# Placing the two kinds of attention score units in pairs instead of one by one, on one core

## The reference

```
xn = layernorm(x)
x1 = x + gqa(xn) + block(xn)         # gqa: 16 query heads, 4 key heads, softmax over 512 keys
   block(xn): r = xn + causal latent attention(rmsnorm(xn))     # 16 heads, causal
              r + moe(rmsnorm(r))                                 # 4 experts, 128 -> 512 -> 128, argmax gate
xn1 = layernorm(x1)
out = x1 + mqa(xn1) + gated_ffn(xn1) # mqa: 16 query heads, one key head; silu(gate) * up, 384 wide
```

## Time and profile before

| | |
|---|---|
| median of three runs | 3557.39 us (3550.87 to 3562.95) |
| profiled execution | 3572.11 us, span 3570.4 us |
| TensorE busy | 3302.7 us, 93% |
| VectorE busy | 2421.1 us, 68% |
| ScalarE busy | 1788.8 us, 50% |
| GpSimd busy | 886.0 us, 25% |
| mean granted TensorE clock | 0.914 |

### The profile page before, as it was taken

The page is one execution under the profiler, slowest core; times in us unless marked ns, Lnnn a source line. Parts: engine busy times, 40 slices in busy tenths (PEclk is TensorE's granted clock), DMA queues, the critical chain, the costliest instruction groups (busy, mean ns, idle before and its releaser), DMA issues.

```text
span 3570.4 us, 72884 instructions
## 1 busy us (share of the span) xinstructions
PE 3302.7 (93%) x18176; PEld 1601.2 (45%) x18176; DVE 2421.1 (68%) x5975; ACT 1788.8 (50%) x3505; POOL 886.0 (25%) x1795
## 2 busy tenths in 40 slices
PE   5899999989999899999999999899998989989987
PEld 2354444535445354453544445354453534535443
DVE  5667676676767767676676766767667676766734
ACT  1625545455454545545455454554545545454544
POOL 3232223212222231222222232122321222222110
PEclk8988999989899898998989899898998989989997
DMA  3010101001010100101001010010101001010000
GB/s 95 14 34 18 44 20 43 15 22 35 19 43 18 30 23 19 44 19 41 11 19 46 19 43 14 22 35 19 43 18 30 23 19 43 18 38 14 16 17 4
DMA packets 69679, 99.17 MB, mean 28 GB/s; under 512 B 7708, under 2 KB 30492, under 8 KB 68944
## 3 DMA queue, kind: packets, MB, share of 16 engines
q1 hardware_dynamic: 69200, 93.66, 10.9%
HBM read 8.59 MB, written 4.19 MB: 4 GB/s over the span
## 4 chain that ended last, share of the span: by engine, by line
PE 84%; DVE 5%; issue 4%; ACT 3%; POOL 2%; POOLq 0%; ACTq 0%; DVEq 0%; DMA 0%; SPq 0%
PE pv L701 19%; PE bank L664 16%; PE bank L683 16%; PE bank L739 7%; PE bank L594 7%; PE bank L747 7%; PE bank L710 3%; ACT probs L1101 2%; PE bank L583 2%; DVE mx L902 2%; PE bank L722 1%; PE bank L626 1%; PE bank L764 1%; POOL sq L1179 1%; PE bank L671 1%
## 5 line engine op out<-in xcount | busy, mean ns | idle before, releaser
L1101 ACT ACTIVATE probs<-bank 128x512 f32<-128x512 f32 x2688 | 1474.5, 598 | 1418.4 <-PE bank L683 1412.1
L902 DVE TENSOR_REDUCE mx<-bank 128x1 f32<-128x512 f32 x2048 | 1300.0, 682 | 304.4 <-PE bank L664 296.5
L909 DVE CUSTOM_DVE_ANT_0 bank<-bank,mask 128x128 f32<-128x128 f32 (+3 forms) x1024 | 486.6, 510 | 208.1 <-PE bank L664 199.2
L1265 POOL TENSOR_SCALAR_AFFINE_SELECT probs<-probs 128x256 f32<-128x256 f32 (+1 forms) x640 | 230.2, 361 | 1050.7 <-ACT probs L1101 1044.9
L664 PE MATMUL bank<-kp_B,qp_B 60*128 60x512 f32 x1024 | 360.1, 471 | 47.8 <-issue 38.9
L664 PE MATMUL bank<-kp_A,qp_A 60*128 60x512 f32 x1024 | 367.4, 484 | 11.3 <-DVE mx L902 8.9
L683 PE MATMUL bank<-qp_B,kp_B 62*128 62x512 f32 x1024 | 355.1, 496 | 2.1 <-ACT probs L1101 2.1
L683 PE MATMUL bank<-qp_A,kp_A 62*128 62x512 f32 x1024 | 322.2, 501 | 7.6 <-DVE mx L902 7.2
L701 PE MATMUL pv<-probs,vv_A 128*32 128x512 f32 x2048 | 307.3, 675 | 23.1 <-ACT probs L1101 23.1
L683 PE MATMUL bank<-qp_M,kp_M 62*128 62x512 f32 (+3 forms) x1024 | 293.4, 373 | 36.1 <-DVE mx L902 34.7
L664 PE MATMUL bank<-kp_M,qp_M 60*128 60x128 f32 (+3 forms) x1024 | 299.5, 374 | 12.6 <-DMA kp_M<-parts_k 6.0
(11 more groups left out here) (144 smaller groups left out, 3298.5 us busy)
## 6 DMA issues: line engine op xcount, KB each, us to landing
qp_M<-parts_q SPq DMA_DIRECT2D x64, 256.0 KB, 4.3
kp_M<-parts_k SPq DMA_DIRECT2D x64, 256.0 KB, 4.3
qp_A<-parts_q SPq DMA_DIRECT2D x64, 256.0 KB, 4.6
qp_B<-parts_q SPq DMA_DIRECT2D x64, 256.0 KB, 3.9
kp_A<-parts_k SPq DMA_DIRECT2D x64, 128.0 KB, 2.6
xs<-x SPq DMA_DIRECT2D x16, 256.0 KB, 2.8
out<-res SPq DMA_DIRECT2D x16, 256.0 KB, 2.3
qp_M<-nmT SPq DMA_DIRECT2D x128, 8.0 KB
```

The costliest lines, as they stand in the source:

```text
L902: v.tensor_reduce(mx[:, g % 2, at:at + 1], s1[BANK[a, g, u]][:], AX.X, ALU.max) \
L909: v.tensor_tensor_reduce(bank[:, 0:keys], bank[:, 0:keys], mask[:, SEQ - keys:SEQ], 1.0, LOWEST, ALU.add, ALU.max, mx[:, g % 2, at:at + 1] ...
L1101: act.activation(probs[:, slot, :], s2[BANK2[a, g, u]][:], ACT.Exp).then_inc(sig[f"{a}_exp"], 1)
L1265: pool.affine_select(out=v, in_=v, compare_op=ALU.is_ge, fill=0.0, base=0, pattern=pattern, channel_multiplier=-1).then_inc(sig["M_masked" ...
```

## The change

Two lines of `stages()` give other times to the score units. Units 2k and 2k + 1 now have one time, for the maxima and for the exponentials; nothing else changes in the text of the kernel.

```
-                put(s + g + u / 16, "score_max", a, g, u)
+                put(s + g + u // 2 / 8 + 0.0313, "score_max", a, g, u)
...
-                put(s + LAG + g + (u + 0.5) / n, "score_exp", a, g, u)
+                put(s + LAG + g + (u // 2 * 2 + 0.5) / n, "score_exp", a, g, u)
```

## The result

The changed kernel took 3360.10 us (median of four runs, 3344.44 to 3369.04); the kernel before, now with a fourth run, 3560.17 us (3550.87 to 3580.83). The ratio is 0.943, with a 95% interval from 0.937 to 0.948: 5.7% faster, 200 us. The forecast had 3430 us and a range down to 3365. The sign was right, the size was not: 130 us were expected.

A forecast was written before the change was run, and what follows sets the result against it. TensorE was taken as the bound, fully so in B's group 3 and M's groups. Savings of 6.1 + 2.1 + 0.4 = 8.6 us a period, by 15, made 129 us: 3430 us, range 3365 to 3530.

The forecast's parts named there:

- 0.23 us for a unit on the fuller half: TensorE: each score unit on a run's fuller array half costs 0.23 us; 501 fewer, 115 us at the full clock.
- The price of a run (0.21): TensorE: having a run of score units at all costs 0.21 us; 379 fewer runs, 80 us.
- B's group 3 and M's groups, 6.1 us a period: Five TensorE-bound stretches at full clock: 14 runs and 20.25 units fewer, 7.6 us, taken at 80%.
- The copy of `pv`, taken as 0: ScalarE, A's and B's 8 groups: copy up to 0.5 us later, offset by a removed unit; bounds 0 to 4.0 us.
- The banks: Ring of 7 banks: pairs leave a bank with its reader 0.50 to 0.61 us longer; room enough, covered by the 20% discount.
- The slower rival: Pairs beside `up`, `down` and projections wait 0.5 us each for unread banks, costing more than saved; 3575 to 3626 us, chance 0.09.
- its smaller brother: Readers eat most: 40 maxima pairs in B's group 3 and M's groups cost 4.9 us a period; 3501 us, chance 0.16.
- A's group 1 and B's group 2, 2.1 us: Stretches mostly at low clock or behind latent-norm work: 2.7 us a period saved, taken at 80%.
- the stretches around the seam and the norm, 0: A's groups 2 and 3, B's groups 0 and 1: set by VectorE, seam and norm chain; upper end 1.8 us.
- the clock a risk upwards alone: TensorE idling longer in A's group 0 could prolong the low clock: 1.5 us a period, 22 in all.
- Rival "more than the rows promise", 3345 to 3370, 0.11: Waits at run starts shrink too, since a pair's second unit stands earlier: whole 12.9 us a period or more; chance 0.11.
- Strict order of the matmuls: Rival: matmuls start in program order, so old runs of 4 and 8 lose a step besides; 3326 us, chance 0.02.

The follow-up runs named there:

- same-half variant: Changed kernel with heads taken 0, 2, 1, 3, so both units of a pair are on the same array half: 3621.67 us, 1.016 of the kernel before.
- the two single changes: Kernel before with only the exponentials in pairs: 3509.35 us, 0.984; with only the maxima in pairs: 3502.17 us, 0.983.
- the variants with fewer runs still: Changed kernel with bursts of four: 3585.27 us, 1.004; with exponential pairs moved next to the maxima pairs: 3377.13 us, 0.946.
- the variant with added matmuls: Kernel before with four more matmuls a period ahead of the transposes of x1, where A's group 1 begins: 3549.82 us, 0.995.
- the control: Kernel before with four extra matmuls a period ahead of the transposes of r2, in B's group 3: 3619.06 us, 1.011.
- the woven variant with the late scaling step: Changed kernel with neighbouring exponential and maxima pairs alternating again, and ScalarE's scaling of the normed input 0.05 later: 3429.41 us, 0.962.
- the woven variant: Changed kernel with neighbouring exponential and maxima pairs alternating again on TensorE, halves 0, 0, 1, 1: 3481.53 us, 0.976.

## Why the prediction was wrong

- **TensorE sets the pace, and only its own work counts**: right. TensorE's busy time fell by 257 us, no other engine's work moved much.
- **0.23 us for a unit on the fuller half**: right, 0.22 in the same-half variant. **A pair costs what one unit cost**: right, 1.43 us. The price of a run (0.21) was not isolated, and may be too high: of the two single changes the maxima, with most of their paper saving in runs (53 of 92 us), fell short (67 us), and the variants with fewer runs still were not faster than the changed kernel.
- **B's group 3 and M's groups, 6.1 us a period**: 5.2 measured. M's four groups gave 5.0, B's group 3 only 0.2, with the new wait of 0.56 us ahead of L710. On their own the pairs in these stretches, with A's groups 2 and 3 and B's group 2, gave 94 us.
- **The copy of `pv`, taken as 0**: nearly. TensorE's wait for it rose from 13.9 us (23 times) to 24.1 us (54 times) over the whole, 10 us. This is one of the signs that I had named for being wrong, too small to matter.
- **The banks**: held. The slower rival and its smaller brother did not happen with pairs.
- **A's group 1 and B's group 2, 2.1 us; the stretches around the seam and the norm, 0; the clock a risk upwards alone**: this is the step that failed. A's group 1, and B's groups 0 and 1, gained 9.9 us together; B's group 2 lost 0.7. I priced their saved work at the full clock and took the clock itself as given, or as something that an earlier idle TensorE could only lose. It is an outcome of the order. In the variant with added matmuls the low stretch around A's group 1 ended sooner with more work in it (a mean of 6.3 us for 14.6); in the changed kernel it is 5.9 us, and pairs in the low stretches alone bring it to 6.8. My reading, not tested by itself, is that the same matmuls stand closer together there.
- **What the clock was worth** is an estimate. In A's group 1, the kernel before had 2 x 0.27 x 25.2 = 13.6 us at 1.2 GHz, the variant with added work 2 x 0.10 x 24.5 = 4.9. It did 3.6 us more work in 0.7 us less, 4.3 us for 8.7 us of low clock, or 0.49 each. The changed kernel has 2 x 0.11 x 19.5 = 4.3 us there: 9.3 x 0.49 = 4.6 of its 5.7 us are the clock's, and the other 1.1 are near the 1.3 to 1.6 that its 3 runs and 3 or 4 units are worth on paper. Over the whole, the variant's rate is (41 + 47) / 240 = 0.37 by its profiled span (3529.2 us at 0.947) with the control's 47 us for the work, and 0.40 with 54. With 0.37 to 0.49, the changed kernel's 230 us less at the low clock are worth 84 to 113 us, and 90 to 119 of the 203 us of its profiled span are left for work and waits, where I had 129. So by this estimate the work was sized a little high, and the clock, put at nothing, was about half of the gain.
- **The parts do not add up exactly.** Paper prices for the work (195 us), 0.40 for each us less at the low clock (92) and TensorE's added idle time (54) make 195 + 92 - 54 = 233 us for the changed kernel, where the spans differ by 203. For the pairs of exponentials alone they make 46 + 44 - 42 = 48 for 61, and for the pairs of maxima alone (0.940 of 3498.1 us, 194 us less at 1.2 GHz) 92 + 78 - 46 = 124 for 72. So the direction of the clock's part is sound and its size is rough.
- A part of the gain was luck in the sense that no sum held it: exponential unit 11 of A's group 3 slipped ahead of ScalarE's scaling step. The prediction counted instructions moved past by TensorE, and looked at ScalarE only around the copy of `pv`. Undone in the changed kernel it costs 23 us.
- **Rival "more than the rows promise", 3345 to 3370 us, 0.11**: had the time, by luck. Its reason, earlier units ahead of their products, is right at that one place only. **Strict order of the matmuls**: its mechanism is refuted by the starts at 0, 0.35, 0, 0.35. Waits do keep the program's order. The Trainium skill's sentence that matmuls are not reordered ("TensorE: Matmul & The Clock Gate", "Part 3: Packing small matmuls — row/col tiling") does not hold for starts between the two row halves in these traces.

What stays open: the 69 us that the woven variant with the late scaling step still lacks, and how much of the clock's part in B's groups 0 and 1 comes from their own runs and how much from other shifts, since B's group 0 had clocks from 0.67 to 0.87 also in variants that changed nothing in it, and work added in A's group 1 shortened its time at 1.2 GHz in the kernel before (9.9 to 4.0 us) and lengthened it in the changed one (7.1 to 10.2).

## What to carry to other kernels

Where the profile shows stretches at a low granted clock, size a change there apart from the rest: ask what it does to the matmul work behind each idle gap, since the time at 1.2 GHz may be worth more than the work. Check such a price against a second variant before trusting it. Small row-tiled matmuls belonged next to each other in pairs on different halves here, two at a time and not four with seven banks in turn. And when steps are moved in a shared table, list for every engine what now stands ahead of each step that waits for a long chain.

## What was not expected of the hardware

- Matmuls on different row halves of the array start out of program order: the third with the first, the second 0.35 us later, in 76 runs of the woven variant behind a product. A third one whose predecessor still waits for its bank is held all the same.
- Adding eight matmul records a period, 3.6 us of work, made the program 0.5% faster (0.991 to 0.998). The granted clock of the stretch with the work went from 0.73 to 0.90, and that of a later stretch, without any, from 0.68 to 0.87.
- One wait of 1.5 us a period, taken away, gave 68 us instead of 23, with the mean clock going from 0.914 to 0.935.
